# Attention on one NeuronCore: scores in 64-row tiles, denominators by DMA, a pipeline through batch ends

## What is computed

```python
Q, K, V = x @ Wq.T, x @ Wk.T, x @ Wv.T          # 16 heads of 16
scores = einsum('bhqd,bhkd->bhqk', Q, K) / 4
lam = 10 * exp(-5 * u_prev)                     # one number per batch
if lam >= 1: softmax over the keys listed (32 indices a query, with repeats)
else:        softmax over all keys, scores + lam * (mask ? 0 : -1)
x = x + (softmax @ V) @ Wo.T + bo
```

## Time and profile before

| | us |
|---|---|
| median of 3 runs | 2168.57 (2167.59 to 2168.61) |
| the profiled execution, its own time | 2169.59 |
| its span, first to last instruction | 2167.9 |
| PE busy | 1993.4 (92%) |
| DVE busy | 1620.8 (75%) |
| ACT busy | 1220.5 (56%) |
| GpSimd (POOL) busy | 776.8 (36%) |

### The profile page before, as it was taken

How to read it: one execution, slowest core, us unless ns; L and a number is a source line. 1 busy time by engine, 2 the same in 40 slices (tenths; PEclk the granted TensorE clock), 3 DMA queues, 4 the chain that set the end, 5 groups by cost and what they waited for, 6 DMA issues and landing times. The chain is left out here.

```text
span 2167.9 us, 42832 instructions
## 1 busy us (share of the span) xinstructions
PE 1993.4 (92%) x14158; PEld 1630.0 (75%) x14158; DVE 1620.8 (75%) x2498; ACT 1220.5 (56%) x2588; POOL 776.8 (36%) x589
## 2 busy tenths in 40 slices
PE   3899999999999999939999999999995999999998
PEld 2566666666666666628888788888875999999997
DVE  6788888888888888857777777777763666666664
ACT  1466666666666666534665665656654555555553
POOL 4644444444444444133333433433320111111111
PEclk8999999999999999969999999999997999999998
DMA  3444444444444444210000000000002222222221
GB/s 94 108 109 107 107 107 107 107 107 107 107 107 107 107 107 107 55 29 1 1 0 0 0 0 0 0 0 0 0 0 88 69 71 87 65 87 66 86 70 59
DMA packets 121175, 137.52 MB, mean 63 GB/s; under 512 B 24240, under 2 KB 89776, under 8 KB 121136
## 3 DMA queue, kind: packets, MB, share of 16 engines
q1 hardware_dynamic: 118576, 128.64, 23.1%
q0 software_dynamic: 2560, 8.39, 1.0%
HBM read 48.35 MB, written 8.39 MB: 26 GB/s over the span
## 5 line engine op out<-in xcount | busy, mean ns | idle before, releaser
L366 DVE TENSOR_REDUCE a_neg_max<-a_s 128x2 f32<-128x512 f32 x512 | 328.9, 682 | 122.8 <-PE a_s L613 121.4
L487 ACT ACTIVATE a_e<-a_t 128x512 f32<-128x512 f32 x512 | 281.1, 610 | 228.1 <-PE a_t L626 228.1
L375 DVE SCALAR_TENSOR_TENSOR a_e<-a_e,a_w_t 128x1024 f32<-128x1024 f32 x256 | 373.3, 1467 | 4.0 <-ACT a_e L487 4.0
L613 PE MATMUL a_s<-a_k_st,a_q_st 96*128 96x256 f32 x1024 | 274.8, 379 | 0.0
L898 POOL TENSOR_TENSOR b_decayed<-b_table,b_mod_t 128x1024 f32<-128x1024 f32 x64 | 127.1, 2007 | 270.6 <-ACT b_mod_t L1169 263.3
L613 PEld LDWEIGHTS a_s<-a_k_st,a_q_st 96*128 96x128 f32 x1024 | 203.2, 198 | 13.5
L1705 ACT ACTIVATE c_hid<-c_pH,c_b 128x256 f32<-128x256 f32 x256 | 107.7, 472 | 187.8 <-PE c_pH L1768 187.3
L610 PE MATMUL a_s<-a_add_m,ident_bf 128*128 128x512 bf16 x512 | 201.5, 394 | 8.0 <-POOL a_add_m L254 5.9
L1329 PE MATMUL b_pS<-b_gated_t,b_decayed 128*128 128x256 f32 x768 | 188.7, 389 | 1.2
L626 PE MATMUL a_t<-a_q_st,a_k_st 97*128 97x512 f32 x512 | 177.2, 427 | 2.8 <-DMA a_q_st<-a_max_row 2.0
L642 PE MATMUL a_v<-a_e,a_v_pad 128*32 128x256 f32 x2048 | 163.4, 392 | 4.5 <-DVE a_e L375 2.1
(11 more groups left out here) (262 smaller groups left out, 5629.4 us busy)
## 6 DMA issues: line engine op xcount, KB each, us to landing
a_q_st<-a_q_hi SPq DMA_DIRECT2D x256, 128.0 KB, 2.4
a_k_st<-a_k_hi SPq DMA_DIRECT2D x256, 64.0 KB, 2.0
a_q_st<-a_q_lo SPq DMA_DIRECT2D x128, 128.0 KB, 2.4
a_xs<-in_xT SPq DMA_DIRECT2D x32, 256.0 KB, 2.8
a_k_st<-a_k_lo SPq DMA_DIRECT2D x128, 64.0 KB, 2.1
x_all<-in_xT SPq DMA_DIRECT2D x32, 256.0 KB, 2.7
c_we<-in_we SPq DMA_DIRECT2D x32, 256.0 KB, 2.7
c_key_t<-in_keyT SPq DMA_DIRECT2D x32, 256.0 KB, 3.1
```

Source lines behind the costliest of these rows:

```text
L366: dve.tensor_reduce(neg_max[:, qc, head:head + 2], ps_s[b][:], AX.X, ALU.max, negate=True).then_inc(red_done, 1)
L375: dve.scalar_tensor_tensor(out=buf[:], in0=buf[:], scalar=BIG, in1=w_t[par][:, kc].unsqueeze(1).to_broadcast([P, 4, S]), op0=ALU.min, op1= ...
L487: act.activation(e[g % E_BUFS][:, 2 * b:2 * b + 2], ps_t[b][:], ACT.Exp).then_inc(exp_done, 1)
L613: ins = pe.matmul(ps_s[b][:, r], q_st[par][0:96, slot, qc * P:qc * P + P], k_st[par][0:96, slot // 2], start=False, stop=(r == 1))
```

## The change

- Scores in 64-row tiles: the three terms take 48 rows (49 with the maximum) in the upper or the lower half of the array. `st` holds q and k of both halves. A group has four row matmuls of 256 columns in pairs r = 0, 1 with `tile_position=(64 * r, 0)`, each r into its own bank; the column scores are four matmuls of 256 in the same way.
- Two pairs of score banks (`ps_s[g % 2]`, two banks each); one reduction of 128x1024 a group. One bank `ps_v`, one `bank`.
- The maxima are turned and placed in halves (`turn_max`, at g = 5 and at g = 0 of the next body); ACT issues their four DMAs (`place_max`).
- `collect` and `spread` on PE, `combine` on DVE go. GpSimd issues nine DMAs a batch instead: denominators to DRAM (2), back as 128x32 (1), merging odd and even heads (4), reciprocals to DRAM (1), spread to 128 rows (1).
- The last two products of a batch move into the next body; `project_out` and `residual` come one and two batches later.
- ACT makes the two parts of the weights, GpSimd adds them; the part of the mask for dense batches goes (all keys there keep their mask in the weights alone).
- GpSimd's long operations wait for a weighing's end (`after_weigh`).
- The constants' block goes, and the counts are summed by 64 matmuls from comparisons in bf16.

```diff
         def score_rows(n, par, g):
-            for b in range(2):
-                    pe.wait_ge(red_done, 2 * (n * GROUPS + g) + b - 1)
-                pe.matmul(ps_s[b][:], ident_bf[:], add_m[par][:, qc].unsqueeze(1).to_broadcast([P, 2, S]), start=True, stop=False)
-                for r in range(2):
-                    ins = pe.matmul(ps_s[b][:, r], q_st[par][0:96, slot, qc * P:qc * P + P],
+                pe.wait_ge(red_done, n * GROUPS + g - 1)
+            for r in range(2):
+                pe.matmul(ps_s[g % 2][:, r], ident_bf[:], add_m[par][:, qc].unsqueeze(1).to_broadcast([P, C, S]), start=True, stop=False)
+            for c in range(C):
                 for r in range(2):
+                    rows = slice(64 * r, 64 * r + 48)
+                    ins = pe.matmul(ps_s[g % 2][:, r, c], st[par][rows, 0, j, c, qc * P:qc * P + P], st[par][rows, 1, j, c],
+                                    start=False, stop=(c == C - 1), tile_position=(64 * r, 0))
...
         def project_k(n, par):
+            pe.wait_ge(qf_done, C * (n + 1))
...
         def body(n, par, proj, maxi, finish):   # tensor
             for g in range(GROUPS):
                 if maxi:
                     score_rows(n + 1, 1 - par, g)
+                if g == 0:
+                    turn_max(n, 1)
+                if g == 5 and maxi:
+                    turn_max(n + 1, 0)
+                score_cols(n, par, g)
                 if g == 0 and proj:
                     project_q(n + 2, par)
                 if g == 1 and proj:
                     project_k(n + 2, par)
-                score_cols(n, par, g)
-                        collect(n - 1)
-                        spread(n - 1)
-                        project_out(n - 1)
-                if maxi and g in (4, 5):
-                    project_v(n + 1, 1 - par, g - 4)
+                if maxi and g in (3, 4):
+                    project_v(n + 1, 1 - par, g - 3)
+                if g in (6, 7) and not (isinstance(n, int) and n < 2):
+                    project_out(n - 2, par, g - 6)
                 if g > 1:
                     mix_values(n, par, g - 2)
-            if maxi:
-                transpose_max(n + 1)
-            mix_values(n, par, GROUPS - 2)
-            mix_values(n, par, GROUPS - 1)
+                elif finish:
+                    mix_values(n - 1, 1 - par, GROUPS + g - 2)
...
         def body(n, par, proj, maxi, finish):   # gpsimd
+                after_weigh(n, 0)
                 masks(n + 2, par)
+                denominators(n - 1, 1 - par, 0)
+                after_weigh(n, 2)
                 weights(n + 1, 1 - par)
+                denominators(n - 1, 1 - par, 1)
+                after_weigh(n, 3)
+                low_part(n + 2, par, 0)
+                compact(n - 1)
+                after_weigh(n, 4)
+                low_part(n + 2, par, 1)
+                merge(n - 1, 1 - par)
+                after_weigh(n, 6)
+                residual(n - 3)
+                reciprocal_rows(n - 1)
+                spread(n - 1)
...
+                if g == 0:                       # scalar, in body
+                    max_rows(n, par, 1)
                 exps(n, g)
+                if g == 0:
+                    place_max(n, par, 1)
+                if g == 0 and maxi:
+                    weight_parts(n + 1, 1 - par)
+                    if g == 0:
+                        whole_q(n + 2)
```

More of the change, by code:

```diff
@@ L198, in _ @@
         stack(1, 1, 0)
-        maxima(0, 0)
         def staged(n, par):
@@ L277, in residual, with low_part @@
+        def low_part(n, par, i):
+            if i == 0:
+                pool.wait_ge(hi_done, n + 1)
+                if not (isinstance(n, int) and n < 2):
+                    for half in d_stack:
+                        pool.wait_ge(half[par], STACK_DMAS * landed(n - 2, par))
+            kind, lo, hi = ((1, 3, 2), (0, 0, 1))[i]
+            pool.tensor_tensor(split[par][:, lo], full[:, kind], split[par][:, hi].bitcast(F32), ALU.subtract).then_inc(lo_done, 1)
         def residual(n):
@@ L297, in _ @@
         masks(0, 0)
-        low_parts(1)
+        masks(1, 1)
         weights(0, 0)
-        masks(1, 1)
         batches(pool, body)
+        for half in range(2):
+            denominators(NB - 1, 1, half)
+        residual(NB - 3)
+        compact(NB - 1)
+        merge(NB - 1, 1)
+        reciprocal_rows(NB - 1)
+        spread(NB - 1)
+        residual(NB - 2)
         residual(NB - 1)
@@ new lines, in score_cols @@
+            if g % 4 == 0:
+                pe.wait_ge(d_max[half], 32 * (n + 1))
+            if not (isinstance(n, int) and n == 0 and g == 0):
+                pe.wait_ge(exp_done, 2 * (n * GROUPS + g))
+            for c in range(C):
+                for r in range(2):
+                    rows = slice(64 * r, 64 * r + 49)
+                    ins = pe.matmul(ps_t[r][:, c], st[par][rows, 1, j, c, kc * P:kc * P + P], st[par][rows, 0, j, c],
+                                    start=True, stop=True, tile_position=(64 * r, 0))
+                    if c == C - 1:
+                        ins.then_inc(t_done, 1)
@@ new lines, in turn_max, with project_out @@
+            ins.then_inc(mt_done[half], 1)
+        def project_out(n, par, m):
+            if m == 0:
+                pe.wait_ge(att_done, n + 1)
+                if not isinstance(n, int) or n + 3 < NB:
+                    pe.wait_ge(mrow_done[0], n + 4)
+                elif n + 3 == NB:
+                    pe.wait_ge(mrow_done[1], NB)
+                else:
+                    pe.wait_ge(delta_done, n)
+            for k in range(C):
+                ins = pe.matmul(bank[:, m], wo[:, k, m * P:m * P + P], att[par][:, k], start=(k == 0), stop=(k == C - 1))
+            if m == C - 1:
+                ins.then_inc(wo_done, 1)
```

647 lines of the change are left out of this document (290 added, 357 removed).

## The result

The changed kernel takes 2068.44 us (median of 4 runs, 2065.91 to 2069.09) against 2168.59 us for the kernel before in the same session: a ratio of 0.9537, 95% interval 0.952 to 0.9553. It is 100 us faster, of 122 us forecast; 2068 lies inside the range given. The profiled execution took 2069.09 us with a span of 2067.2, 100.5 us less than the profiled one before. First its busy times over the whole span, then those of the steady part of the attention stage (columns as in the earlier trace rows).

What follows compares the result with a forecast made beforehand. The prediction took PE's stream to bind the attention stage, DVE 3.6 us behind. Batches -107, setup -15, last bodies -4 and -4, tail +8: -122 us, from 2169.6 to 2047.6 (2047 against the median); range 1985 to 2120.

Steps and rivals of the forecast that it cites:

- PE's own work: TensorE's work per batch in the attention stage: 25.9 - 3.0 - 1.8 + 0.8 + 0.6 = 22.5 us.
- six pieces by 0.1: +0.6: Projections on PE now lie behind a 64-row block; six pieces each pay a 0.1 us switch, +0.6 us a batch.
- 26.96 less about 1 of waits: PE's work per batch in the kernel before: the 26.96 us beat less about 1 us waiting, 25.9 us.
- The interlock: PE up to the rows of g = 2, five DVE iterations without a gap, then the product: 23.4 us a batch.
- PE stands 1.1 us: Ahead of the key projection, PE waits 1.1 us for ACT's query copy, since both projections use one bank.
- The weighings: On DVE: near 1.2 us each, without the 2 us ones, as GpSimd's operations start at a weighing's end.
- rival C: The stack's DMAs are late each batch, behind SP's and GpSimd's queues: 24.1 to 25 us a batch, 2068 to 2095; 15%.
- Setup: Before the loop: comparisons in bf16 -12, leading block some -6, part given back by 36 stack issues; taken -15 us.
- -8 for the last bodies and +8 for the tail: Stage end: body without projections -4, last body without denominators' matmuls -4; tail's four dependent DMAs 12.5 us instead of 5, +8.
- A (DVE alone): DVE alone sets the attention stage's beat, ACT's issues costing little: 21.2 us a batch, 1981 us; 14%.
- B (pairs do not run at once): The paired 64-row score matmuls on PE do not overlap: 25.8 us a batch, 2120 us; 16%.
- D (GpSimd held up by DVE): Each of GpSimd's nine DMA issues waits out a DVE weighing: 29.3 us a batch, 2224 us, slower; 6%.

Runs made afterwards that it cites:

- the kernel drained at batch ends: The changed kernel with the last two products and the last weighing put back at each batch's own end; 2129.67 us, ratio 0.9819.
- the variant of the kernel before: The kernel before with collecting matmuls for the denominators cut from eight to one and spreading ones from four to one; 2140.32 us, ratio 0.9862.

## Why the prediction was right, and where it was off

**The bound** was read rightly: PE's stream before, and PE's stream after. Halving the reductions moved the beat by 0.06 us. The beat itself, 23.4 forecast, is 23.60, but that is luck in part: PE's own work was taken 0.8 us too small, and a stand of 1.1 us was added that is not there, while another of 0.3 us is.

**PE's own work** was mis-sized: 22.5 us forecast, 23.3 measured (23.6 less the 0.3 that the query projection waits for the turned maxima's copy). The plain group was close (2.07 - 0.23 = 1.84 forecast, 1.78 measured), and the turned maxima too (0.51 by 2, 0.8 forecast on top of 0.3). The wrong term is "six pieces by 0.1: +0.6". A half projection has 0.77 us of streaming (1.54 / 2) and costs 1.06, so 0.29 for cutting it into tiled work; the query projection takes 1.89 us of the stream (514.09 to 515.98) and the key projection 1.93, against 1.54. Together 4 x 0.29 + 0.35 + 0.39 = 1.9 us, where 0.6 was forecast behind the same streaming. The price of 0.1 had come from a column-tiled product with loads of 32 columns, the only row there was; the pieces load 128 columns, most likely with nothing to cover the first load. Of the 1.3 us by which this term was short, the plain groups give back 8 x 0.06 = 0.5. The base of that sum, "26.96 less about 1 of waits", had no row either: PE's idle time before is 0.4 us a batch (338.00 less 333.33 over 12.54 batches).

The Trainium skill (TensorEngine Tiling (Array Packing), Key Properties) says that a change of tiling mode drains the engine; the trace agrees in that a visit costs: 0.29 us for a half projection, 0.20 of it saved when the piece stood next to other full-array work. How much of it is a drain and how much an uncovered load, no row tells.

**The interlock.** "PE stands 1.1 us" ahead of the key projection was wrong. It starts at 517.76, right behind the column scores. The forecast had ACT's query copy end 6.4 us behind the row scores of g = 0; it ends at 5.5 (517.56 - 512.07), since the two DMA issues run beside the exponentials and cost 0.3 us between them, not 1.26, and PE gets there at 5.7, later than the 5.3 forecast. Moving the weight parts changed nothing, which settles it. So the sum behind it (9.5 + 13.3 + 0.57) is not the beat. DVE's wait of 2.12 and 1.35 us for the row scores of g = 1 and 2 was as described, but there is slack at the other end. The wait that the one bank does cause was overlooked: the query projection's, for the copy of the turned maxima, 0.3 us.

**DVE.** The weighings came out as forecast, 1.29 us on the mean (1.47 before), at most 1.66 in the batch shown, but not by the ties that the forecast gave as the reason: without them the mean is 1.25. What shortened them is open. Without the ties it is the normalization that suffers, 2.0 us, which the forecast did not name.

**The late stack,** rival C, is real but stands in one place: 29 batches by 23.60 would be 684.4 us, the trace has 689.96, so 5.6 us over the stage. 3.3 of it are the two batches in the middle (1.6 the late stack, 1.7 the clock's fall), the rest lies in the first six, where PE's waits for the stack come to only 0.8 us. Rival C was given 15% as a lasting state, by the length of SP's and GpSimd's queues; what makes the stack late here is GpSimd's one pause.

**The ends.** Setup gave 9.6 us of 15. The comparisons were 0.2 us each as taken, and row scores start at 41.25, not 37; the 36 stack issues by 0.64 last until 52.2. Forecast -8 for the last bodies and +8 for the tail; measured -6.5 (0.6 - 7.1) and +7.1: the tail from the last raw copy (813.54) to the last residual is 18.0 us, before 10.9. The 3.8 us behind it were not forecast at all.

**The rivals.** A (DVE alone) failed because PE's sum is above DVE's. B (pairs do not run at once) is false by the start times. D (GpSimd held up by DVE) is false as a lasting state: its issues take 0.58 to 0.62 us, and four in a row 1.96; whether the one pause of 2.75 us has to do with DVE is open.

The sum, with sizes as measured: -95.4 for 29 batches (forecast 30 by 3.56 = 107), of which the beat gives 100.9 (785.34 less 29 by 23.60) and the irregular batches take 5.6; setup -9.6; end +0.6; the next stage's start +3.8.

## What to carry to other kernels

When four resources lie within 1 us of each other, removing work from one buys only the distance to the next: taking 0.8 to 4.3 us from TensorE's work in the changed kernel bought nothing, and 0.25 us a batch once `delta` had two buffers; splitting the one bank was not tried. Find the shared buffer whose release closes the second chain before shortening the first. And price a switch between full-array and tiled work by a piece of the same form (1.06 us between tiled work, 0.86 beside full-array work), not by the cheapest switch in the trace.

## What the runs showed of the hardware that was not expected

**A stand of PE can cost the clock.** After 1.6 us of waiting in 4.9, the query projection ran at a granted clock of 0.53 and took 3.65 us instead of 1.96: in the kernel without mask matmuls, where it takes 3.4 to 3.8 us in every batch from the eighth on, and in the changed kernel once behind the late stack and twice in the first six batches (3.25 and 3.40 us). A kernel that makes PE less busy can so gain nothing. But it is not the stand alone. With the order within the pairs turned, the same stand of 1.60 us at the same place left the clock at 1.00, and so did 2.0 us a batch, in pieces of up to 0.7, in the steady part of the kernel drained at batch ends. What decides is not shown by these runs.

**Matmuls of two row tiles run two at a time however they are issued:** both orders gave starts within 10 ns in twos, and the same time. By the semaphores of the column scores the two are one of each tile, so the engine starts them in another order than the program's.

**GpSimd's queue is slow to close a stage once it has issued DMAs.** Between the last residual and the next stage lie 4.27 us instead of 0.50; the record inside is one drain instruction of 3.82 us, 0.05 before. The drain is 3.82 us in all eleven variants of the changed kernel, and 0.05 in the variant of the kernel before. That it is the DMAs is argued from the two kernels alone; no run took them away.

**A GpSimd operation that is running when a two-input DVE operation starts** can stretch it, by what it has left less 0.13 us: 0.68 where the residual had 0.80 left (509.90 + 1.28 - 510.38), 0.45 where it had 0.58 (the weighing of 1.66 at 511.50 in the changed kernel), and 0.89 before, at 518.23, where the low part had 1.02. Not every operation does, and the other way round it is GpSimd's that grows: the normalization at 505.03 kept its 0.68 us while the low part that started 0.17 us into it took 1.65 instead of 1.26. A weighing that starts while GpSimd issues a DMA keeps its 1.21 us. The normalization behind four issues, with the residual next, grew by 2.02 and ended 0.56 us after the residual; why it did not finish before the residual began is open. The reduction kept its 1.2 us throughout.
